# Experts of a routed layer computed on sorted tokens instead of on all tokens for every expert

## The chip, the cores and the metric

One core of one Trainium2 chip runs one program. The time is device microseconds (us) from its first to its last instruction, as the runs report it. The kernel before takes 6748.31 us (median of 3 runs, 6740.82 to 6760.65).

## What is computed

The input has 16 batches of 1024 tokens with 29 features; every token becomes 128 numbers (float32). Two layers follow. Layer 0 is attention with 8 heads of 64 after a group norm, and a small MLP over the channels. Layer 1 is attention with 8 heads of 16, and then the routed part, which is what the change touches:

```python
logits = xf @ switch_w.T + switch_b            # 16 experts
route_probs = max(softmax(logits)); routes = argmax(...)
pos = rank of the token among all tokens (of all batches so far) with its expert
keep = pos < capacity                          # int(1.2 * 16384 / 16)
y = buf @ expert_w[e].T + expert_b[e]          # 128 -> 128, by the token's own expert e
out = where(keep, y[routes, pos], xf) * route_probs
h = h + out
```

## The kernel before

**Batches are pipelined.** The program has five stages: `first` (layer 0 of batch 0), `second` (layer 0 of batch 1 beside layer 1 of batch 0), `loop` (13 passes: layer 0 of batch i+2, layer 1 of batch i+1, and the routed part of batch i), `penult` (the same without a new batch) and `final` (layer 1 of the last batch beside the routed part of the last but one). After `final` the routed part of the last batch runs alone, the tail. The stage `second` has no routed part; otherwise it does what a pass of `loop` does.

**Steps.** An attention unit is one head by one half (512) of the queries; it has 8 steps, each a score product of a key tile (L909, L911), its exponential on ScalarE (L1141) and a share of the products with the values (L930, L931 in layer 0, L946 in layer 1). A pass of `loop` has 32 units, layer 1 and layer 0 in turn, so 256 steps. Everything else is laid beside the steps by hand: each helper is a generator that yields the step at which its next piece is due, and every engine's program is written out in the order of the steps (`Beside.run(step)`). So each engine executes its queue strictly in this order; a wait anywhere holds up all that is behind it on that engine.

**What stands around the change.** The row maxima of the scores are worked out first (products L883 into two banks, reductions on VectorE L1640), turned to a row (L889, L1130), and the row goes into the stack of queries by a DMA from SyncE (`row`, L600), at steps that are multiples of 8. SyncE also issues the stacks of each head: `stack0` three DMAs of 512 KB (L569) at steps 64, 96, 128 and 160 among others, `stack1` five smaller ones at steps 56, 88, 120 and 152. All DMAs are issued by SyncE, on one hardware queue. GpSimd makes the low halves of the probabilities of layer 0 (`lo_parts`, L508), three at kt 2, 4 and 6 of a layer-0 unit and one at kt 0 of the next unit, which TensorE needs from kt 2 of that unit on.

**The routed part** (`switch`, one for each engine) turns and normalizes the tokens (steps 18 to 31), forms the logits, the one-hot `oh` and the rank (`rank`, `place`), and the weight `wgt` = one-hot times kept probability. The expert weights `ewT` (16 x 128 x 128) lie in SBUF throughout. The experts run at steps 64 to 191 of a pass, two pieces every 8 steps:

```python
mm(bank[:, :], mT[:, t * P:(t + 1) * P], ewT[:, 4 * q:4 * q + 4, :]...)      # L869, 32 of them
dve.scalar_tensor_tensor(hm[:, t, :], bank[:, e * P:(e + 1) * P],
                         wgt[:, t, ...], hm[:, t, :], ALU.mult, ALU.add)      # L1630, 128 of them
```

that is, every token tile goes through all 16 experts, and VectorE adds each result times its weight, which is zero for all but one expert. Small products go through two shared PSUM banks (`glue`), whose uses alternate in the order of their steps (`glue_plan`, `use`, `await_filled`, `await_drained`). In `final` a step is shorter, and three expert pieces stand in 16 steps. Step numbers of the routed part are in `switch_slots`; the store of `hm` is at step 191 (124 in `final`), L662 and L665.

## Time and profile before

| | |
|---|---|
| median of 3 runs | 6748.31 us |
| the profiled execution | 6749.96 us, span 6748.1 us |
| granted TensorE clock, mean | 0.948 |
| busy: PE, DVE, ACT, POOL | 90%, 67%, 48%, 37% |
| one pass of `loop` (256 steps) | 402 to 410 us |
| the stage `second` (256 steps) | 371.9 us |
| `final`, then the tail | 185.4 us, 123.3 us |

Stage and step boundaries are the starts of the exponentials L1141 in the trace, one a step: the pass that the rows below use begins at 1987.5 us and ends at 2389.7 us, and its step 64 is at 2095.5, step 80 at 2116.0, step 96 at 2136.2. Of `second`, step 0 is at 396.7, step 64 at 494.8, step 80 at 513.6, step 192 at 660.2. A window that begins and ends at such times shows what a number of steps cost, and the same steps of `second` and of `loop` can be laid side by side.

### The profile page before, as it was taken

How to read it: one execution, taken by the hardware profiler on the slowest of the kernel's cores; microseconds unless marked ns; L12 is line 12 of the kernel's file. 1: busy time of each engine (PE TensorE's matmuls, PEld its weight loads, DVE VectorE, ACT ScalarE, POOL GpSimd, SP SyncE). 2: the span in 40 equal slices, each digit the busy share in tenths (PEclk: the TensorE clock that was granted, in tenths of full speed). 3: DMA queues.
4: the chain of work that ended last, by engine and by line, in shares of the span. 5: the costliest groups of instructions: out<-in, count | busy, mean ns of one | idle time of the engine just before them, and what ended most of it. 6: DMA issues, size and time to landing. Idle time of an engine off the chain costs nothing.

```text
span 6748.1 us, 127182 instructions
## 1 busy us (share of the span) xinstructions
PE 6073.5 (90%) x40167; PEld 4046.7 (60%) x40167; DVE 4525.4 (67%) x11162; ACT 3214.0 (48%) x6321; POOL 2465.6 (37%) x2215
## 2 busy tenths in 40 slices
PE   6789898998989989898998989989898998989986
PEld 4656665656656666665656656666665656656643
DVE  4466676676767767676776767767676776767664
ACT  2345555445444444544545445444544445454541
POOL 2534333433333333333433333333333433333300
PEclk7899999999999999999999999999999999999987
DMA  2121211212222121211212222121211212221110
GB/s 60 41 68 42 59 42 38 64 39 53 49 55 48 40 50 45 59 42 38 64 40 52 49 55 49 40 50 45 59 42 38 64 33 59 49 54 42 25 30 9
DMA packets 98048, 317.03 MB, mean 47 GB/s; under 512 B 27782, under 2 KB 32854, under 8 KB 87126
## 3 DMA queue, kind: packets, MB, share of 16 engines
q1 hardware_dynamic: 97366, 308.41, 19.7%
q8 instruction: 370, 6.06, 0.4%
q14 instruction: 312, 2.56, 0.1%
HBM read 57.19 MB, written 41.94 MB: 15 GB/s over the span
## 4 chain that ended last, share of the span: by engine, by line
issue 47%; POOL 27%; PE 17%; DVE 6%; DMA 1%; POOLq 1%; ACT 1%; SPq 1%; DVEq 0%; ACTq 0%
POOL pr_lo L508 22%; PE bank L883 3%; POOL on L1264 3%; PE bank L911 2%; PE bank L869 2%; PE bank L946 2%; DVE mxh L1640 2%; PE bank L930 1%; DMA stacks<-parts 1%; PE bank L931 1%; DVE z L1428 1%; POOL rs L1235 1%; PE bank L793 1%; PE bank L909 1%; PE bank L956 1%
## 5 line engine op out<-in xcount | busy, mean ns | idle before, releaser
L1640 DVE TENSOR_REDUCE mxh<-bank 128x1 f32<-128x512 f32 x4096 | 2789.9, 687 | 1710.2 <-PE bank L883 1682.2
L1141 ACT ACTIVATE pr<-bank 128x512 f32<-128x512 f32 x4096 | 2419.4, 598 | 2713.8 <-PE bank L911 2669.6
L883 PE MATMUL bank<-stacks 128*128 128x512 f32 x4096 | 2225.5, 544 | 335.2 <-DVE mxh L1640 231.8
L508 POOL TENSOR_TENSOR pr_lo<-pr 128x1024 bf16<-128x1024 f32 x960 | 1824.3, 1901 | 1168.9 <-ACT pr L1141 1168.6
L911 PE MATMUL bank<-stacks 65*128 65x512 f32 (+1 forms) x4096 | 1667.7, 407 | 5.0 <-ACT pr L1141 5.0
L883 PEld LDWEIGHTS bank<-stacks 128*128 128x128 f32 x4096 | 801.3, 196 | 1122.2 <-DVE mxh L1640 804.7
L930 PE MATMUL bank<-v,pr 128*128 128x129 bf16 x8192 | 1079.9, 224 | 54.1 <-POOL pr_lo L508 53.5
L931 PE MATMUL bank<-v,pr_lo 128*128 128x129 bf16 x8192 | 1067.7, 222 | 0.0
L930 PEld LDWEIGHTS bank<-v,pr 128*128 128x128 bf16 x8192 | 787.9, 99 | 348.4 <-issue 306.3
L1264 POOL TENSOR_TENSOR on<-on,o_r 128x128 f32<-128x128 f32 x512 | 235.3, 460 | 2015.7 <-DVE on L1670 2015.6
L911 PEld LDWEIGHTS bank<-stacks 65*128 65x128 f32 (+1 forms) x4096 | 801.6, 196 | 225.0 <-issue 61.7
L909 PE MATMUL bank<-stacks 128*128 128x512 f32 x2048 | 834.4, 407 | 0.2 <-ACT pr L1141 0.2
L931 PEld LDWEIGHTS bank<-v,pr_lo 128*128 128x128 bf16 x8192 | 813.4, 99 | 0.0
L869 PE MATMUL bank<-ewT,mx 128*128 128x512 f32 x1024 | 585.4, 658 | 114.1 <-DVE hm L1630 44.8
L1630 DVE SCALAR_TENSOR_TENSOR hm<-bank,wgt,hm 128x128 f32<-128x128 f32 x2048 | 570.5, 342 | 52.5 <-PE bank L869 52.5
L946 PE MATMUL bank<-pr,v 128*32 128x512 f32 x4096 | 547.0, 609 | 0.0
L909 PEld LDWEIGHTS bank<-stacks 128*128 128x128 f32 x2048 | 402.6, 197 | 131.8 <-ACT pr L1141 77.7
L869 PEld LDWEIGHTS bank<-ewT,mx 128*128 128x128 f32 x1024 | 185.8, 204 | 236.5 <-DVE hm L1630 69.3
L956 PEld LDWEIGHTS bank<-fold,oT 128*128 128x128 f32 x2048 | 272.6, 200 | 60.3 <-ACT oT L1158 46.7
L1041 ACT ACTIVATE parts<-bank,cols 128x512 fp32r<-128x512 f32 x256 | 176.4, 689 | 228.2 <-PE bank L721 228.0
L956 PE MATMUL bank<-fold,oT 128*128 128x32 f32 x2048 | 266.0, 275 | 12.5 <-ACT oT L1158 12.5
L1272 POOL TENSOR_TENSOR on<-on,o_r 128x64 f32<-128x64 f32 x256 | 75.2, 294 | 519.2 <-DVE on L1682 519.1
(171 smaller groups left out, 5070.9 us busy)
## 6 DMA issues: line engine op xcount, KB each, us to landing
stacks<-parts SPq DMA_DIRECT2D x384, 512.0 KB, 6.5
stacks<-parts_d SPq DMA_DIRECT2D x224, 128.0 KB, 3.0
parts_d<-mx SPq DMA_DIRECT2D x16, 1024.0 KB, 4.5
stacks<-parts_d SPq DMA_DIRECT2D x224, 64.0 KB, 2.8
stage<-in_pe SPq DMA_DIRECT2D x16, 512.0 KB, 8.0
stacks<-mrow SPq DMA_DIRECT2D x512, 2.0 KB
parts_d<-on SPq DMA_DIRECT2D x16, 512.0 KB, 5.3
parts_d<-stage SPq DMA_DIRECT2D x16, 512.0 KB, 6.2
```

Source lines behind the costliest of these rows:

```text
L508: return eng.tensor_tensor(low_of(u, kt - 1).rearrange("p a b -> p (a b)"), w, hi, ALU.subtract)
L869: mm(bank[:, :], mT[:, t * P:(t + 1) * P], ewT[:, 4 * q:4 * q + 4, :].rearrange("p e f -> p (e f)"), start=True, stop=True).then_inc(fille ...
L883: mm(maxb[k % 2][:, :], qs[:, t * P:(t + 1) * P], ks[:, g * HALF:(g + 1) * HALF], start=True, stop=True).then_inc(max_filled.sem, 1)
L909: mm(bank[:, :], kA[:, head % 2, kk], qA[:, head % 2, q], start=True, stop=False)
L911: mm(bank[:, :], k_stack(layer, head)[0:last, kk], q_stack(layer, head)[0:last, q], start=(layer == 1), stop=True).then_inc(score_filled.s ...
L930: mm(dst, hi, v0[:, head // 2 % 2, kt, head % 2, 0:w], start=(kt == 0), stop=False)
L931: last = mm(dst, lo, v0[:, head // 2 % 2, kt, head % 2, 0:w], start=False, stop=(kt == T - 1))
L946: last = mm(obank[n % 2][QUAD * r:QUAD * (r + 1), :], v1[:, kt, col:col + QUAD], pr[:, at % 2, kt, :], start=(j == 0), stop=(j == 1))
L956: last = mm(obank[n % 2][:, QUAD * t:QUAD * (t + 1)], oT[:, t * P:(t + 1) * P], fold[:, :], start=True, stop=True)
L1141: act.activation(pr[:, at % 2, kt, :], score[k % 2][:, :], ACT.Exp, scale=SCALES[layer]).then_inc(exp_done.sem, 1)
L1630: ins = dve.scalar_tensor_tensor(hm[:, t, :], bank[:, e * P:(e + 1) * P], wgt[:, t, 4 * q + e:4 * q + e + 1], hm[:, t, :], ALU.mult, ALU.add)
L1640: dve.tensor_reduce(mxh[:, layer, n // 2, n % 2:n % 2 + 1], maxb[k % 2][:, :], AX_X, ALU.max)\
```

## The change

The tokens of a batch are sorted by expert through memory. Every expert gets whole tiles of 128 slots, at most 24 tiles in all. VectorE works out from the counts how many tiles each expert has, where they begin, each token's slot and each tile's expert number (`tables`, `place` + 2). GpSimd scatters the 8 tiles of tokens to `x_sort_d` by 8 indirect DMAs. In 6 groups of 4 tiles, SyncE loads the sorted tokens, TensorE turns them and multiplies each tile by the weights of its one expert, VectorE copies the result and SyncE stores it to `y_sort_d`. GpSimd gathers each token's result by 8 indirect DMAs, and VectorE adds it times the kept probability. The weights now lie in memory (`ew_d`, written at the start); SyncE reads a tile's expert number from SBUF into a register (`value_load`) and loads that expert's 64 KB into a ring of 8. `x_sort` and `y_sort` are the halves of `z`, `y_own` is `mT`.

```diff
@@ switch_slots, of a pass of loop (final: 23, 28, 35, group 42, sums 112 and 118)
+              "logits": 36, "route": 38, "rank": 44, "tables": 46, "place": 54, "wT0": 59, "wT1": 60, "eb0": 62, "eb1": 63, "scatter": 65}
+        group, sums = 74, (148, 156)
+    at.update({f"{name}{g}": group + 12 * g + step for g in range(GROUPS)
+               for name, step in (("load", 0), ("slots", 3), ("product", 5), ("weights", 8), ("store", 9))})
@@ SyncE, before the first load of x
+                sp.dma_start(ew_d.rearrange("e d f -> d e f"), ewT).then_inc(prep_out, 16)
+                for n in range(3):
+                    sp.dma_start(x_sort_d[n * S:(n + 1) * S, :].rearrange("(t p) c -> p t c", p=P),
+                                 stacks1[:, n % 2, 1, :].rearrange("p (t c) -> p t c", t=T).bitcast(F32)).then_inc(prep_out, 16)
@@ SyncE, switch
+                def load_weights(g):
+                    for j in range(4 * g, 4 * g + 4):
+                        e = sp.value_load(tile_ei[0:1, j:j + 1], min_val=0, max_val=E - 1)
+                        sp.dma_start(wring[:, j % 8, :], ew_d[e]).then_inc(weights_in[g % 2].sem, 16)
+                for g in range(2):
+                    yield AT["tables"] + 4 + 2 * g
...
+                    load_weights(g)
+                for g in range(GROUPS):
+                    yield AT[f"load{g}"]
+                    if g == 0:
+                        await_all((scattered.sem, scattered.at(b, 16 * T)))
+                    else:
+                        await_all(drained(seg, f"{pre}slots{g - 1}"))
+                    sp.dma_start(x_sort, x_sort_d[4 * g * P:4 * (g + 1) * P, :].rearrange("(t p) c -> p t c", p=P))\
+                        .then_inc(x_sort_in.sem, 16)
+                    yield AT[f"weights{g}"]
+                    await_all(drained(seg, f"{pre}product{g}"))
+                    if g + 2 < GROUPS:
+                        sp.nop(nofuse=True)
+                        load_weights(g + 2)
+                    yield AT[f"store{g}"]
+                    sp.dma_start(y_sort_d[4 * g * P:4 * (g + 1) * P, :].rearrange("(t p) c -> p t c", p=P), y_sort)\
+                        .then_inc(y_sort_out.sem, 16)
@@ TensorE, switch
-                for n in range(16):
-                    for d in range(2):
...
-                        mm(bank[:, :], mT[:, t * P:(t + 1) * P], ewT[:, 4 * q:4 * q + 4, :].rearrange("p e f -> p (e f)"),
-                           start=True, stop=True).then_inc(filled, 1)
+                for g in range(GROUPS):
+                    yield AT[f"slots{g}"]
+                    te.wait_ge(x_sort_in.sem, x_sort_in.at(b, 16 * (g + 1)))
+                    turn(seg, f"{pre}slots{g}", lambda j: x_sort[:, j, :])
+                    yield AT[f"product{g}"]
+                    te.wait_ge(weights_in[g % 2].sem, weights_in[g % 2].at(b, 64 * (g // 2 + 1)))
+                    bank, filled = use(seg, f"{pre}product{g}", f"{pre}slots{g}")
+                    for j in range(4):
+                        at = g % 2 * HALF + j * P
+                        last = mm(bank[:, j * P:(j + 1) * P], mT[:, at:at + P], wring[:, (4 * g + j) % 8, :], start=True, stop=True)
@@ ScalarE: moves the turned tiles (slots0 to slots5) to mT, one more wait (y_sort_out) at oT0.2.0
@@ GpSimd, switch
+                    if t == 0:
+                        pool.wait_ge(slot_ready.sem, slot_ready.at(b, 1))
+                    pool.indirect_dma_start(x_sort_d, bass.IndirectOffsetOnAxis(slot_i[:, t:t + 1], 0), z[:, t, :], None)\
...
+                    if t == 0:
+                        pool.wait_ge(y_sort_out.sem, y_sort_out.at(b, 16 * GROUPS))
+                    pool.indirect_dma_start(y_own[:, t, :], None, y_sort_d, bass.IndirectOffsetOnAxis(slot_i[:, t:t + 1], 0))\
@@ VectorE, switch: 11 small operations of tables, 4 of slots, then
+                    bank, drained = await_filled(dve, seg, f"{pre}product{g}")
+                    if g > 0:
+                        dve.wait_ge(y_sort_out.sem, y_sort_out.at(b, 16 * g))
+                    dve.tensor_copy(y_sort, bank_tiles(bank)).then_inc(drained, 1)
...
+                        dve.wait_ge(y_own_in.sem, y_own_in.at(b, 16 * T))
+                    ins = dve.scalar_tensor_tensor(hm[:, t, :], y_own[:, t, :], kr[:, t:t + 1], hm[:, t, :], ALU.mult, ALU.add)
-STORE_STEPS = {"loop": 191, "penult": 191, "final": 124}
+STORE_STEPS = {"loop": 163, "penult": 163, "final": 126}
```

## Rows read from the trace of the kernel before

**Rows 1.** Windows, busy time of each engine: stage second, one pass of loop.
```profile
396.70:768.60 371.90, 337.74 (x2370) 228.59 (x2369) 235.46 (x514) 196.19 (x388) 150.67 (x127) 0.97 0.22 51
1987.50:2389.70 402.20, 371.04 (x2510) 249.47 (x2510) 282.21 (x696) 200.78 (x395) 154.10 (x138) 0.97 0.21 49
```
**Rows 2.** Windows, steps 64 to 191: second, then loop.
```profile
494.80:660.20 165.40, 154.02 (x1109) 102.22 (x1108) 102.37 (x222) 88.12 (x182) 71.39 (x61) 0.98 0.23 52
2095.50:2279.70 184.20, 176.66 (x1173) 113.76 (x1172) 135.79 (x352) 88.58 (x181) 70.35 (x59) 0.99 0.21 50
```
**Rows 3.** Windows of 16 steps: second 80, loop 80, second 96, second 128.
```profile
513.60:532.40 18.80, 17.57 (x132) 11.57 (x130) 11.64 (x25) 10.14 (x23) 8.62 (x8) 1.00 0.07 22
2116.00:2136.20 20.20, 20.20 (x140) 13.14 (x139) 15.83 (x41) 10.16 (x23) 8.62 (x8) 1.00 0.07 21
532.40:552.00 19.60, 18.38 (x140) 12.40 (x139) 11.81 (x25) 11.16 (x24) 9.05 (x9) 1.00 0.46 110
574.50:595.70 21.20, 19.43 (x148) 13.36 (x146) 13.61 (x28) 11.21 (x25) 8.61 (x7) 1.00 0.37 76
```
**Rows 4.** Groups of instructions: count, busy us, mean ns, idle before.
```profile
L869 PE MATMUL bank<-ewT,mx 128*128 128x512 f32 x1024 | 585.4, 658 | 114.1 <-DVE hm L1630 44.8 <-DVE parts L1440 26.4 <-DVE stage L1435 22.4
L1630 DVE SCALAR_TENSOR_TENSOR hm<-bank,wgt,hm 128x128 f32<-128x128 f32 x2048 | 570.5, 342 | 52.5 <-PE bank L869 52.5
L1384 DVE COPY ewT<-bank 128x512 f32<-128x512 f32 x4 | 2.5, 682 | 7.3 <-PE bank L693 7.3
L1574 DVE TENSOR_TENSOR lg<-bank,sb_b 128x128 f32<-128x128 f32 x16 | 4.7, 291 | 14.7 <-PE bank L846 14.7
```
**Rows 5.** Timeline of SyncE at steps 96 to 100: start, us, line.
```profile
2136.94 0.67 SPq L600 DMA_DIRECT2D stacks<-mrow  x1
2137.76 3.24 SPq L569 DMA_DIRECT2D stacks<-parts  x3
2141.26 2.17 SPq L638 DMA_DIRECT2D stage<-in_pe  x1
```
**Rows 6.** Windows around these transfers; last columns clock, DMA share, GB/s.
```profile
2139.00:2149.00 10.00, 10.00 (x91) 7.27 (x88) 8.09 (x22) 5.00 (x11) 1.59 (x3) 1.00 0.90 212
2149.00:2157.00 8.00, 8.00 (x51) 4.93 (x50) 6.18 (x18) 4.57 (x9) 5.09 (x4) 1.00 0.00 0
```
**Rows 7.** DMA issues: count, KB each, median us from issue to landing.
```profile
xin<-in_x SPq DMA_DIRECT2D x16, 116.0 KB, 2.1
stacks<-parts_d SPq DMA_DIRECT2D x224, 128.0 KB, 3.0
stage<-in_pe SPq DMA_DIRECT2D x16, 512.0 KB, 8.0
```
**Rows 8.** Timeline of GpSimd around a layer-1 unit: start, us, line.
```profile
2116.24 1.89 POOL L508 TENSOR_TENSOR pr_lo<-pr 128x1024 bf16<-128x1024 f32 x1
2128.00 1.89 POOL L508 TENSOR_TENSOR pr_lo<-pr 128x1024 bf16<-128x1024 f32 x1 [1.32 <-ACT pr L1141]
```
**Rows 9.** Timeline of the start: the load of x, its first reader.
```profile
33.99 0.37 SPq L565 DMA_DIRECT2D xin<-in_x  x1
36.12 1.88 PE L710 MATMUL bank<-tri_sb,xin 128*29 128x128 f32 x8 [8.45 <-DMA xin<-in_x]
```
**Rows 10.** Windows of final (64 steps with experts, 15 without), and the tail's experts.
```profile
6511.60:6608.50 96.90, 81.05 (x376) 40.58 (x376) 69.00 (x186) 41.36 (x81) 2.34 (x8) 1.00 0.06 17
6608.50:6624.80 16.30, 14.26 (x75) 6.29 (x79) 7.64 (x27) 9.47 (x20) 0.59 (x2) 1.00 0.09 33
6658.70:6745.10 86.40, 52.76 (x64) 15.74 (x62) 34.58 (x129) 0.00 (x0) 0.00 (x0) 0.63 0.00 0
```
**Rows 11.** Timeline of the tail: start, us, line; idle before.
```profile
6630.55 3.37 PE L838 MATMUL bank<-wo_sb,mx 128*128 128x128 f32 x16 [0.18 <-ACT mx L1025]
6639.33 1.12 PE L710 MATMUL bank<-tri_sb,z 128*128 128x128 f32 x4 [0.48 <-DVE z L1428]
6652.28 2.18 DVE L1607 SCALAR_TENSOR_TENSOR hm<-z,small,hm 128x128 f32<-128x128 f32 x8
```

More of the change, by code:

```diff
@@ L202, in switch_slots @@
     if kind == "final":
-        at = {"oT1.0": 1, "oT1.1": 2, "attn1.0": 5, "attn1.1": 6, "ln.0": 7, "ln.1": 8, "z.0": 9, "z.1": 10, "zT3.0": 11, "zT3.1": 13, "logits": 15,
-              "route": 16, "rank": 21, "place": 24, "wT0": 29, "wT1": 30, "eb0": 32, "eb1": 33}
-        first = [37 + 16 * m + s for m in range(6) for s in (0, 3, 8)][:16]
+        at = {"oT1.0": 1, "oT1.1": 2, "attn1.0": 5, "attn1.1": 6, "ln.0": 7, "ln.1": 8, "z.0": 9, "z.1": 10, "zT3.0": 11, "zT3.1": 13,
+              "logits": 15, "route": 16, "rank": 21, "tables": 23, "place": 28, "wT0": 33, "wT1": 34, "eb0": 36, "eb1": 37,
+              "scatter": 35}
+        group, sums = 42, (112, 118)
     else:
         at = {"oT1.0": 18, "oT1.1": 19, "attn1.0": 21, "attn1.1": 22, "ln.0": 22, "ln.1": 24, "z.0": 26, "z.1": 28, "zT3.0": 30, "zT3.1": 31,
-              "logits": 36, "route": 38, "rank": 44, "place": 54, "wT0": 59, "wT1": 60, "eb0": 62, "eb1": 63}
-        first = [8 * m for m in range(8, 24)]
-    return {**at, **{f"e{n}.{d}": s + d for n, s in enumerate(first) for d in range(2)}}
-NO_BANK = ("route", "place", "copy", "res0", "gn", "xn", *(f"{name}.{g}" for name in ("ln", "z", "ln1", "z1", "ln2", "z2") for g in range(2)))
+              "logits": 36, "route": 38, "rank": 44, "tables": 46, "place": 54, "wT0": 59, "wT1": 60, "eb0": 62, "eb1": 63, "scatter": 65}
+        group, sums = 74, (148, 156)
+    at.update({f"{name}{g}": group + 12 * g + step for g in range(GROUPS)
+               for name, step in (("load", 0), ("slots", 3), ("product", 5), ("weights", 8), ("store", 9))})
+    return {**at, "gather": sums[0], "sum": sums[1]}
+NO_BANK = ("route", "tables", "place", "scatter", "gather", "sum",
+           *(f"{name}{g}" for name in ("load", "weights", "store") for g in range(6)), "copy", "res0", "gn", "xn", *(f"{name}.{g}" for name in ("ln", "z", "ln1", "z1", "ln2", "z2") for g in range(2)))
 def glue_plan(kind):
@@ L561, in _ @@
                     .then_inc(ones_in, 16)
+            store_prep()
             sp.wait_ge(ones_in, 32)
@@ L652, in segment @@
                     load_x(seg.nxt)
+                if seg.kind == "second":
+                    sp.wait_ge(prep_out, 64)
+                beside = [Beside(switch(seg, "", seg.sw))] if seg.sw else []
                 for step in range(LAST[seg.kind]):
@@ L659, in segment @@
                         load_positions(seg, seg.nxt)
+                    for work in beside:
+                        work.run(step)
                     if seg.sw and step == STORE_STEPS[seg.kind]:
-                        await_drained(sp, seg, "e15.1")
+                        await_all((hm_ready.sem, hm_ready.at(seg.sw, 1)))
                         sp.dma_start(out_v[seg.sw.index()], hm[:, :, :]).then_inc(out_stored.sem, 16)
                 if seg.kind == "final":
-                    await_drained(sp, seg, "f.e15.1")
+                    Beside(switch(seg, "f.", seg.l1)).run(LAST_STEP)
+                    await_all((hm_ready.sem, hm_ready.at(seg.l1, 1)))
                     sp.dma_start(out_v[seg.l1.index()], hm[:, :, :]).then_inc(out_stored.sem, 16)
@@ L1123, in switch @@
                     move_T(seg, f"{pre}wT{g}", xT[0:E, g * HALF:(g + 1) * HALF], E)
+                for g in range(GROUPS):
+                    yield AT[f"slots{g}"]
+                    move_T(seg, f"{pre}slots{g}", half(mT, g % 2))
             def max_rows(seg, name, b, layer, head, g):
@@ L1571, in switch @@
                 top, total, rp, vm, pos, kr, un = (small[:, n, :] for n in range(7))
+                own, tiles, begin, shift = (counts[:, n, :] for n in range(4))
                 yield AT["logits"]
```

129 lines of the change are left out of this document (95 added, 34 removed).

## The prediction

> **What bounds the kernel now.** I read the busy time by stage first. A pass of `loop` keeps TensorE busy for 371 of 402 us, VectorE for 282, GpSimd for 154 [rows 1]; TensorE is the bound, and its queue is in order, so any wait in it is lost unless it falls into the 31 us that are idle. Then I laid `second`, which has no routed part, beside `loop`: 371.9 against 402.2 us. Over steps 64 to 191, where only the experts differ, it is 165.4 against 184.2 us (from 184 to 187 in the passes of `loop`) [rows 2]. That is the ceiling: with the experts gone altogether a pass gains about 20 us; `second` gives about 2 us of it back in the next 16 steps, so I use 19. Busy time would promise more: L869 is 585 us (36.6 a batch) and L1630 570 us (35.7) [rows 4]. But in 16 plain steps four expert products cost 1.4 us of time (20.2 against 18.8), because `second` leaves TensorE 1.2 us idle there [rows 3]. Most of VectorE's relief is worth nothing: it was never the bound.
>
> **Part by part, for one pass of `loop`.**
>
> *Removed*, 32 products and 128 additions: -19 us, as above (bounds -17 and -21).
>
> *TensorE's new work*, 6 groups. Turning four tiles: 16 steps of `second` with two turns more cost 19.6 against 18.8, so 0.4 us a turn. Four products of 128x128 have the form of a value chunk: two of these cost 21.2 - 18.8 = 2.4, so 1.2 us each [rows 3]. 6 x 1.6 = 9.7 us; I take off 3 that falls into idle time, as the experts' did: +6.5.
>
> *VectorE and ScalarE*: six copies of 0.68 and about 15 small operations, the larger ones at 0.29 to 0.6 by L1574 [rows 4]: some 4 us of tables in one place, steps 46 to 57, where the maxima behind them wait: +1.5. Six moves of ScalarE: +0.5. Together with TensorE +8.5; without any wait a pass would gain 10.5.
>
> *Waits for transfers.* This decides. TensorE waits in its queue for the sorted tokens at `slots`, 3 steps after SyncE's `load`, and SyncE has to get there through its own queue. The length of a step here is 1.2 us (18.8 / 16).
>
> Two prices are not in the trace. (a) A register read with its weight DMA. SyncE's issue of a plain DMA takes 0.37 [rows 9], and 0.67 [rows 5]; the read is a round trip, which costs from nothing to the 2.1 us of the smallest load shown [rows 7]. So 0.5 to 2.7 us a pair; I take 1.35 (nearer the bare issue, since no data engine is started for the read), so W = 5.4 us for four. The Trainium skill (DMA: Bandwidth & Descriptors, Latency and other measured facts) states a floor of some 0.6 us for a register load; no run here shows it, and by it W would be 4.4 at least, and the total lower by some 15 us. (b) An indirect DMA on GpSimd, d: from 0.37 (a plain issue of SyncE) to 1.9 (GpSimd's 128x1024 operation [rows 8], which handles far more elements); I take 1.2, the middle, since no row is near it, and keep both ends.
>
> - Group 2 is the worst. Its load is due at step 98, and at step 96 `stack0` issues three DMAs of 512 KB [rows 5]. All go through one queue, and it is full: from 2139 to 2149 us the DMA share is 0.90 at 212 GB/s, then 0.00; these 10 us are the stacks with the 512 KB of positions behind them, which take 8.0 us to land where 128 KB alone take 3.0 [rows 6, 7]. The load of 256 KB, put before the positions, lands at about 2139 + 1.8 MB / 207 KB per us + 0.5 = 2148.3. TensorE wants it at step 101, 2136.2 + 5 x 1.22 = 2142.3: it waits 6 us even if nothing else is late. Further `weights1` is due at step 94, 2.4 us before the stack: W = 5.4 and the store's 0.5 put the row and the stack of step 96 later by about 3 us, and so the load. 9.5 us.
> - Group 1: from `weights0` (82) to `slots1` (89) there are 8.5 us; W + 0.5 (store) + 3.2 (issue and landing) = 9.1: 0.5 us. Groups 4 and 5 stand behind the stacks of 120 and 128: 1 us each. Group 3: nothing.
> - Group 0: from `scatter` (65) to `slots0` (77) there are 14.8 us; 8d + 2.5 (landing) + 3.0 = 15.1: 0.5 us. GpSimd itself has the gap for it: 9.9 us between L508 of step 72's unit and the next [rows 8], against 9.6.
> - Gather (148) to sum (156): 9.6 us; 8d + 2.5 = 12.1, so VectorE stands still for 2.5 and behind it the maxima; TensorE has two banks of them in hand: 1.5 us. The low halves due from step 154 come about 2.5 us late and catch up, since they wait 1.3 us each for exponentials anyway [rows 8].
>
> Together 14 us. A rule speaks against the first of these. The row: 1.5 MB of stacks and 0.5 MB of positions hold the queue for 10 us [rows 6]. The Trainium skill (the same page, Anatomy of one DMA) fits a DMA as 2.0 us plus its bytes at 436 GB/s; by that 1.8 MB would be through in some 4 + 2 us and the wait would be 4 us shorter, the total then by some 55 us. The measured rate is half of that, and I go by it.
>
> One pass: -19 + 8.5 + 14 = +3.5 us; 13 passes: +45. `penult` has no positions to load but is otherwise alike: +4.
>
> *`final`*: 64 steps with experts take 96.9 (24.2 for 16), without 16.3 for 15 (17.4 for 16) [rows 10]: 88 steps give -37. New: 9.7 of TensorE, 1.5 of tables; scatter (35) to `slots0` (45) has 11.3 us against 15.1: 4; gather to sum has 6.8 against 12.1: 5; behind weights and the stacks of 48 and 64: 8. Sum -9.
>
> *Tail*, where nothing hides anything. Before, from `wgt` (6652.3) to 6745.1 us: 93 us [rows 10, 11]. After: tables and slots 2.5, L1607 2.2, scatter 8d + 2.5 = 12.1; each group: issue and landing 3.1, turn 1.1, move 0.6, product 1.7 (half of L838), copy 0.7, store 0.4, hand-overs 0.5 = 8.1, six times 49; four times W = 21.6; then 2.7 + 9.6 + 2.5 + 2.2 = 17. Sum 104: +11.
>
> *Start*: `store_prep` puts 1 + 1.5 MB on the queue in front of the load of x, which TensorE waits for within 2.1 us of its issue [rows 9]. At 207 KB per us this is 12 us, with 2 of issue: +14 (10 to 18). The 48 small memsets of VectorE lie in its wait for the first loads.
>
> **Sum**: 45 + 4 - 9 + 11 + 14 = +65 on the profiled execution's 6750, which stands 2 us above the median: 6815 us.
>
> **Rivals.**
>
> 1. *The transfers hide* (faster). The load of group 2 isn't held up to the end, since the stacks' transfers are done before the positions are, or the steps before it run late enough anyway; register reads are cheap (W = 3). Then the waits are 2 us a pass: -8.5 x 14 = -119; `final` -20, tail 0, start +10: 6621. For it: the ceiling of 20 us is measured, and TensorE loses 17 us of work. Against it: 212 GB/s and the step numbers. The Trainium skill's rate (above) leads the same way, if only to about 6760.
> 2. *GpSimd and SyncE take the place of the wait* (slower still). With W = 9 (2.2 a pair) and d = 1.9: group 0 waits 6, group 1 4, group 2 13, group 4 5, gather 7: 35 us, so +24 a pass. 14 passes +340, tail +40, start +14: 7145. It decides from d above 1.3, where the scatter no longer fits in its 12 steps, and from W above 5, where `weights` reaches the next load. For it: 24 reads and 16 indirect DMAs a pass, each in an in-order queue. Against it: SyncE's issues are short.
> 3. *It doesn't do what it says*: the routed part is off TensorE's path, and the change is worth nothing there. `second` against `loop` speaks against it (19 us). Start and tail alone would give 6773.
>
> **How the numbers follow.** The forecast 0.42 (its own range 6770 to 6900), rival 1 0.32 (6560 to 6750), rival 2 0.18 (6900 to 7400), rival 3 0.08. The bounds of (a) and (b) put a pass between -4 and +35; with the other cases the range is 6600 to 7090. A measurement of this kernel can tell 0.3% (20 us) from no change. Faster by more: rival 1 and a little of the forecast's lower end, 0.33; within: 0.09; slower: 0.58.
>
> **What would show it.** Right: TensorE idle before the turn of group 2 for about 9 us, released by the DMA of `x_sort`; the same turn in groups 0 and 1 with under 1 us; a pass of `loop` of 405 to 412 us; about 20 fewer busy us of TensorE and 25 of VectorE in it; x landing 14 us later at the start; a tail of 104 us after `wgt`. Wrong: no DMA among the releasers of the turns, and steps 64 to 191 in less than 178 us (rival 1); GpSimd's indirect DMAs over 1.5 us each or SyncE over 2 us for a weight tile (rival 2); the load of group 2 landing in 3 us though the stacks are under way.

## The result, and the profile after

The changed kernel takes 6996.52 us (median of 4 runs, 6990.53 to 7008.85) against 6751.26 us of the kernel before beside it: a ratio of 1.0366, 95% interval 1.0345 to 1.0387. It is slower. It lies inside the full range of 6600 to 7090, but outside the forecast's own (6770 to 6900): slower by 245 us where 65 were forecast. By stages (profiled executions, starts of the exponentials as boundaries, us):

| stage | before | after | difference | forecast |
|---|---|---|---|---|
| start | 84.0 | 92.8 | +8.8 | +14 |
| `first` and `second` | 684.6 | 679.1 | -5.5 | 0 |
| 13 passes of `loop` | 13 x 405.3 | 13 x 422.3 | +220 | +45 |
| `penult` | 401.3 | 421.6 | +20.3 | +4 |
| `final` | 185.4 | 174.3 | -11.1 | -9 |
| tail | 123.3 | 131.3 | +8.0 | +11 |

So nearly the whole miss lies in the passes: 16.9 us each where 3.5 were forecast. (The change doesn't touch the work of `first` and `second`; over the kernels below these take 677.5 to 684.4 us, so their -5.5 is scatter.) The windows of the pass that answers to [rows 1 to 3], of the kernel after: the whole pass, steps 48 to 63, steps 64 to 191, steps 80 to 95 (from, to, length, busy time and count of PE, PEld, DVE, ACT, POOL, granted clock, DMA share, GB/s).

```profile
2035.40:2456.20 420.80, 366.15 (x2518) 251.88 (x2518) 264.26 (x596) 204.26 (x401) 170.24 (x154) 0.94 0.26 61
2117.60:2148.40 30.80, 26.23 (x176) 17.70 (x176) 25.03 (x59) 13.77 (x28) 12.86 (x16) 0.96 0.11 31
2148.40:2344.70 196.30, 171.02 (x1181) 116.35 (x1180) 111.31 (x236) 92.03 (x188) 84.86 (x74) 0.92 0.31 74
2172.70:2192.50 19.80, 18.81 (x145) 12.85 (x143) 12.70 (x27) 10.67 (x23) 7.81 (x7) 1.00 0.23 64
```

TensorE is busy 5 us less than before and VectorE 18 less (about 20 and 25 were forecast), and the pass is longer: TensorE's idle time rose from 31 to 55 us. The granted clock adds to it: TensorE was at the lower of its two levels (1.2 GHz) for 697 us of the program before and for 1124 us now, in stretches behind its waits. The calm window of steps 80 to 95 costs 19.8 us, less than the 20.2 with the experts [rows 3]. The table of waits of the kernel after says where the idle time begins (who waits, for whom, us in all, times, longest):

```profile
PE bank L788 <- DMA z<-x_sort_d: 225.8, 68, 12.2
PEld bank L788 <- DMA z<-x_sort_d: 191.8, 54, 12.5
ACT pr L1229 <- remote: 127.2, 37, 6.2
DVE mxh L1771 <- remote: 124.6, 32, 6.7
PE bank L1012 <- POOL pr_lo L541: 86.7, 120, 3.6
```

The first two lines were forecast: the turns wait for sorted tokens. The next two were not: ScalarE and VectorE, which here wait for TensorE's products (the scores, and those whose maxima are taken), stand still up to 6.7 us, and the profile knows no releaser for the wait ("remote" is its word for a signal that it can't place; there is one core). The kernel before has no such line.

*Group 2*, SyncE's queue and then TensorE's, kernel after (start, us, line; idle before in brackets), beside [rows 5]:

```profile
2190.79 3.69 SPq L687 DMA_DIRECT2D wring<-ew_d  x4
2194.53 0.44 SPq L709 DMA_DIRECT2D y_sort_d<-z  x1
2195.09 0.71 SPq L641 DMA_DIRECT2D stacks<-mrow  x1
2195.98 3.27 SPq L610 DMA_DIRECT2D stacks<-parts  x3
2199.37 2.31 SPq L701 DMA_DIRECT2D z<-x_sort_d  x1
2201.94 2.13 SPq L679 DMA_DIRECT2D stage<-in_pe  x1
```
```profile
2206.65 1.12 PE L788 MATMUL bank<-tri_sb,z 128*128 128x128 f32 x4 [7.43 <-DMA z<-x_sort_d]
```

Four register reads with their weight DMAs take 4.6 us (forecast 5.4, bounds 2 to 10.8): the 3.69 us of the row begin with the first DMA, and the read in front of it begins at 2189.85. A read takes 0.27 us (median of 384), a pair 1.12. The load comes behind the three stacks, as worked out, and TensorE stands for it. The signs that were named for this came true: before the turn of group 2 TensorE waits 7.4 us a pass for `x_sort`, before that of group 0 not at all, before that of group 1 0.9 us.

*The scatter*, GpSimd, VectorE and ScalarE of the kernel after, at steps 64 to 72. Here is the new thing:

```profile
2146.50 1.89 POOL L541 TENSOR_TENSOR pr_lo<-pr 128x1024 bf16<-128x1024 f32 x1
2148.56 1.09 POOL L1387 DMA_INDIRECT x_sort_d<-z,slot_i  x1 [0.17 <-issue]
2149.95 0.97 POOL L1387 DMA_INDIRECT x_sort_d<-z,slot_i  x1 [0.30 <-issue]
...
2155.03 0.96 POOL L1387 DMA_INDIRECT x_sort_d<-z,slot_i  x1 [0.30 <-issue]
2158.78 0.40 POOL L1353 TENSOR_TENSOR on<-on,o_r 128x128 f32<-128x128 f32 x1 [2.80 <-DVE on L1801]
```
```profile
2152.63 0.69 DVE L1771 TENSOR_REDUCE mxh<-bank 128x1 f32<-128x512 f32 x1 [2.03 <-issue]
2157.42 0.69 DVE L1771 TENSOR_REDUCE mxh<-bank 128x1 f32<-128x512 f32 x1 [4.11 <-remote]
```
```profile
2153.01 0.60 ACT L1229 ACTIVATE pr<-bank 128x512 f32<-128x512 f32 x1 [2.08 <-PE bank L993]
2157.46 0.60 ACT L1229 ACTIVATE pr<-bank 128x512 f32<-128x512 f32 x1 [3.85 <-remote]
```

Six indirect DMAs follow each other 1.27 us apart (d, forecast 1.2). While they run, VectorE and ScalarE both wait some 4 us for products of TensorE and go on within 0.04 us of each other. VectorE's product was the first of these, done at 2154.12 by the profile, 3.3 us before VectorE goes on; the two last products of this kind, which start at 2154.19 and 2154.42, were done 2.6 us before:

```profile
2153.65 0.47 PE L965 MATMUL bank<-stacks 128*128 128x512 f32 x1
2154.19 0.39 PE L965 MATMUL bank<-stacks 128*128 128x512 f32 x1
2154.42 0.40 PE L993 MATMUL bank<-stacks 128*128 128x512 f32 x1
```

GpSimd itself is not what they wait for: it is idle for 2.80 us at the end, waiting for VectorE.

The trace also holds the times at which the engines' signals (semaphore increments) were seen, and they say what is late. TensorE's are seen 0.01 us behind the product (median). Here five of them, of products that ended from 2153.84 to 2154.82, are seen between 2157.37 and 2157.50, one every 0.03 us: held, then let go together. Each of the 4096 reductions of VectorE (L1771) belongs to one product of TensorE (L965), so they can be paired. In the kernel after, 41 of them start more than 1 us after both their product and their engine were ready, 6.5 us at most. In the kernel before the longest such delay is 0.1 us. (The ends of products are modelled by the profile, but 0.1 and 6.5 us come from the same model.)

*Start* and *tail*, kernel after: SyncE's stores, then TensorE's first wait, which was 8.45 us [rows 9]. From the last `wgt` (6885.8 us) to the end (6988.7) it is 102.9 us; 104 were forecast.

```profile
33.38 0.45 SPq L592 DMA_DIRECT2D ew_d<-pr  x1
33.87 5.36 SPq L594 DMA_DIRECT2D x_sort_d<-stacks  x3
39.27 1.79 SPq L606 DMA_DIRECT2D xin<-in_x  x1
```
```profile
44.88 1.88 PE L788 MATMUL bank<-tri_sb,xin 128*29 128x128 f32 x8 [16.72 <-DMA xin<-in_x]
```

### The profile page after: what moved, and what is told of

Its sections match the earlier page's. It is cut to its first block, busy times and chain, and to the rows that moved or that the text cites. A ratio compares the mean times of both kernels' runs of the same rounds, so it can differ in the third digit from the quotient of the medians.

```text
span 6988.7 us, 127660 instructions
## 1 busy us (share of the span) xinstructions
PE 5958.0 (85%) x40295; PEld 4084.1 (58%) x40295; DVE 4223.4 (60%) x9610; ACT 3271.9 (47%) x6417; POOL 2725.3 (39%) x2471
## 3 DMA queue, kind: packets, MB, share of 16 engines
q0 software_dynamic: 8192, 16.79, 0.9%
## 4 chain that ended last, share of the span: by engine, by line
issue 46%; POOL 29%; PE 14%; DVE 5%; DMA 2%; SPq 2%; ACT 1%; POOLq 1%; another core or an unknown queue 0%; DVEq 0%; ACTq 0%
POOL pr_lo L541 21%; PE bank L965 3%; POOL on L1353 2%; PE bank L993 2%; DVE mxh L1771 2%; POOL x_sort_d L1387 1%; PE bank L1028 1%; POOL mx L1395 1%; PE bank L1012 1%; DMA stacks<-parts 1%; DVE z L1540 1%; PE bank L1013 1%; PE bank L871 1%; POOL rs L1324 1%; PE bank L991 1%
## 5 line engine op out<-in xcount | busy, mean ns | idle before, releaser
L1771 DVE TENSOR_REDUCE mxh<-bank 128x1 f32<-128x512 f32 x4096 | 2773.9, 687 | 2147.4 <-PE bank L965 1974.9
L965 PE MATMUL bank<-stacks 128*128 128x512 f32 x4096 | 2122.3, 519 | 507.3 <-DVE mxh L1771 387.0
L993 PE MATMUL bank<-stacks 65*128 65x512 f32 (+1 forms) x4096 | 1712.1, 418 | 11.2 <-DMA stacks<-mrow 5.0
L965 PEld LDWEIGHTS bank<-stacks 128*128 128x128 f32 x4096 | 823.5, 201 | 1284.6 <-DVE mxh L1771 965.5
L1012 PE MATMUL bank<-v,pr 128*128 128x129 bf16 x8192 | 1104.4, 227 | 88.8 <-POOL pr_lo L541 86.7
L1013 PE MATMUL bank<-v,pr_lo 128*128 128x129 bf16 x8192 | 1092.4, 225 | 2.7 <-issue 2.7
L993 PEld LDWEIGHTS bank<-stacks 65*128 65x128 f32 (+1 forms) x4096 | 827.4, 202 | 174.5 <-issue 37.4
L991 PE MATMUL bank<-stacks 128*128 128x512 f32 x2048 | 852.1, 416 | 9.4 <-ACT pr L1229 5.3
L991 PEld LDWEIGHTS bank<-stacks 128*128 128x128 f32 x2048 | 412.4, 201 | 86.0 <-ACT pr L1229 41.8
L788 PE MATMUL bank<-tri_sb,z 128*128 128x128 f32 x768 | 146.9, 323 | 237.5 <-DMA z<-x_sort_d 225.8
L1038 PEld LDWEIGHTS bank<-fold,oT 128*128 128x128 f32 x2048 | 290.3, 210 | 61.7 <-ACT oT L1246 45.1
L1107 ACT ACTIVATE mx<-bank 128x512 f32<-128x512 f32 (+1 forms) x256 | 152.7, 597 | 368.5 <-PE bank L788 367.5
L1038 PE MATMUL bank<-fold,oT 128*128 128x32 f32 x2048 | 281.2, 284 | 12.5 <-ACT oT L1246 12.5
L788 PEld LDWEIGHTS bank<-tri_sb,z 128*128 128x128 f32 x768 | 106.0, 165 | 297.6 <-DMA z<-x_sort_d 191.8
```

Of the source, the lines that this page charges most:

```text
L788: last = te.transpose(bank[0:rows_, j * P:(j + 1) * P], src(j), ident)
L965: mm(maxb[k % 2][:, :], qs[:, t * P:(t + 1) * P], ks[:, g * HALF:(g + 1) * HALF], start=True, stop=True).then_inc(max_filled.sem, 1)
L991: mm(bank[:, :], kA[:, head % 2, kk], qA[:, head % 2, q], start=True, stop=False)
L993: mm(bank[:, :], k_stack(layer, head)[0:last, kk], q_stack(layer, head)[0:last, q], start=(layer == 1), stop=True).then_inc(score_filled.s ...
L1012: mm(dst, hi, v0[:, head // 2 % 2, kt, head % 2, 0:w], start=(kt == 0), stop=False)
L1013: last = mm(dst, lo, v0[:, head // 2 % 2, kt, head % 2, 0:w], start=False, stop=(kt == T - 1))
```

## Experiments

Since all engines run in the order of the steps, I lay the start times of the exponentials, step by step and as a mean over the 13 passes, beside those of the kernel before without its experts. A cost then shows as a jump at a step and stays. "At 96 to 104" means: between these steps.

### 1. The ceiling, and what the indirect DMAs add to it

```diff
 e1_b_noexperts, from the kernel before
-                for n in range(16):          (TensorE's L869, VectorE's L1630)
 e2_b_noexp_indirect: e1, and on GpSimd, waited for by no other engine
+                first, second = (35, 112) if seg.kind == "final" else (65, 148)
+                for t in range(T):           (two a step)
+                    pool.indirect_dma_start(ind_d, ...ind_i[:, t:t + 1]..., ind_sb[:, t, :], None)
+                for t in range(T):           (the same from ind_d to ind_sb at second)
```

> The kernel before without its expert products and their additions (L869, L1630), the rest of the routed part kept; it leaves the expert outputs out of the result. It measures the ceiling. If second against loop is a fair picture (my forecast's 19 us a pass), steps 64 to 191 take about 165 us and the whole about 6751 - 14 x 19 - 40 (final) - 85 (tail) = 6360 us. If TensorE's relief is partly taken back by later waits (rival), a pass gains 10 us or less and the whole is above 6480.

> The same kernel with 8 indirect scatters and 8 indirect gathers on GpSimd at steps 65 and 148 of a pass (35 and 112 in final), to and from a buffer of their own that no engine reads; nothing waits for them. Theory hold-up: indirect DMAs in flight hold up TensorE's completions by themselves (the trace of the changed kernel shows exponentials and maxima idle 3 to 6 us with no releaser, about twice a batch): 8 us a pass and some slow clock behind, so 110 to 200 us above e1. Theory waits: only what waits for the transfers costs time, GpSimd has room: within 20 us of e1.

Without the 32 products and 128 additions: 6360.57 us (ratio 0.9417, 0.9402 to 0.9433), a pass 18.3 us shorter than before (forecast 19). With 16 indirect DMAs a batch beside it, of data that nobody reads: 6543.39 (0.9685, 0.9665 to 0.9704), a pass 12.0 us longer again. The ledger has two jumps, +4.6 us at 64 to 72 and +7.3 at 152 to 160, the places of the two eights. The waits of this kernel show the lines without a releaser, which e1 has not:

```profile
ACT pr L1141 <- remote: 135.7, 47, 5.3
DVE mxh L1640 <- remote: 137.2, 33, 6.7
```

So it is the indirect DMAs that hold the engines up, whatever their data are for. Paired as above, 37 reductions of e2 are held for over 1 us, the longest for 6.4 us. In e1 none is held for more than 0.1 us.

### 2. The changed kernel without its indirect DMAs, and with earlier loads

```diff
 e3_a_noindirect
-                    pool.indirect_dma_start(x_sort_d, ...)   and the gather's; their signals are given at once
 e4_a_loads_early, SyncE's switch
-               for name, step in (("load", 0), ("slots", 3), ...
+    at.update({f"load{g}": group + (12 * g - 7 if g else 0) for g in range(GROUPS)})
+                    if g + 1 < GROUPS:
+                        yield AT[f"load{g + 1}"]
+                        load(g + 1)          (ahead of weights g and store g)
```

> The changed kernel without its 16 indirect DMAs a batch; their semaphores are raised by GpSimd itself, so the sorted tokens are not the batch's. Theory hold-up: it gains what e2 loses to e1, 8 us a pass or more, plus VectorE's wait for the gather (2 to 3 us): 6996 - 14 x 11 - 30 (final and tail) = about 6810. Theory waits: it gains only VectorE's wait and the late scatter, 3 to 4 us a pass: about 6925.

> The changed kernel with the load of group g+1 issued 2 steps after the turn of group g (7 steps earlier than in the change), so ahead of the weights, the store and the stacks of steps 96, 120 and 128. Theory waits for sorted tokens: the 11 us at steps 100 to 104 and the 4 us at 136 to 140 go, with the slow clock behind them: 14 x 14 = -190, about 6800. Rival (a wait moved, not removed: the queue is the bound and the stacks or the rows come later): under 5 us a pass, above 6930.

e3: 6892.52 us (1.0218, 1.0201 to 1.0235), 104 us less than the kernel after. That is nearer to the second theory (6925) than to the first (6810). The hold-up is gone nevertheless: no wait without a releaser is left, the wait for group 2 is (10.6 us at 96 to 104), and so is that of group 5 (5.8 at 136 to 144). e4 is the counterpart: 6765.76 us (1.0018, 1.0008 to 1.0029). Both jumps are nearly gone (1.3 and 0.9 us are left), a pass is 15.0 us shorter, and the waits for sorted tokens fall from 225.8 us to these (e4, the whole program):

```profile
PE bank L795 <- DMA z<-x_sort_d: 29.9, 6, 12.3
```

One edit of seven steps in SyncE's queue thus takes back nearly all that the change had cost. The jumps of +4.7 at 64 to 72 and +7.9 at 152 to 160 stay in e4. In e3 they are -0.1 and +2.1, the latter from the sum at step 156, where the kernel after has 3.5 and 8.0. Of these 9.5 us e3 gives 3 back behind step 160, and its pass is 6.5 us shorter where the first theory wanted 8 or more and VectorE's wait on top.

### 3. What of an indirect DMA holds the engines up

Four kernels from e1, with 16 operations of GpSimd a batch each:

```diff
 e5_b_noexp_gpsimd_busy: additions, at the steps of e2
+                        link(seg, pool.tensor_tensor(ind_sb[:, 4:7, 0:110], ind_sb[:, 0:3, 0:110], ind_sb[:, 0:3, 0:110], ALU.add))
 e6_b_noexp_plain_dma: plain addresses, at the steps of e2
+                    pool.dma_start(ind_d[t * P:(t + 1) * P, :], ind_sb[:, t, :])
 e7_b_noexp_ind_quiet: e2 at other steps
+                first, second = (35, 112) if seg.kind == "final" else (81, 177)
 e8_b_noexp_ind_spread: e2, one in three steps
+                    yield first + (t if seg.kind == "final" else 3 * t)
```

> The kernel before without its experts (6360.6) with 16 additions of 128x330 on GpSimd a batch, about 1.0 us each, at the steps where the run with indirect DMAs (6543.4) had its 16: same time taken on GpSimd, no DMA. Theory QUEUE (the indirect DMAs cost by the 0.96 us that each holds GpSimd, behind which low parts and normalizations are late): 6520 to 6560, the same +12 us a pass. Theory PATH (what holds up TensorE, ScalarE and VectorE is how the indirect DMAs reach the rest of the chip, not GpSimd's time): 6360 to 6410, at most 3 us a pass, and no waits of ScalarE or VectorE without a releaser.

> The same 16 transfers of 64 KB a batch at the same steps, issued by GpSimd too, but with plain addresses in place of indices. If any transfer issued by GpSimd at these steps holds the engines up (PATH, all kinds): 6500 to 6550. If only the indirect ones do, by reading indices and writing 128 addresses each (PATH, indirect): 6365 to 6400. QUEUE expects the issue time on GpSimd times 16 in ratio to 0.96 us: with 0.3 us each 6400 to 6430.

> The kernel before without its experts with the 16 indirect DMAs moved from steps 65 and 148 to steps 81 and 177 of a pass, packed as they were. At 81 and 177 GpSimd is busy 7.8 of 20 and 11 of 24 us (15 of 24 and 16 of 27 at the old places, with the indirect ones in it) and at 177 no stack is under way. QUEUE: the low parts have slack there, 6400 to 6460. PATH with contention for the DMA engines: half of it left, 6440 to 6480. PATH without: as before, 6530 to 6560.

> The kernel before without its experts with the 16 indirect DMAs of a batch one every three steps from steps 65 and 148 (in the last segment one a step), in place of two a step. QUEUE: 0.96 us at a time fits between the low parts, 6370 to 6420. PATH with a fixed hold-up for each DMA (0.75 us each of the 12 us a pass): 6530 to 6560. PATH with a hold-up that builds up only where they queue: 6380 to 6440, which this run does not tell from QUEUE, but the run with additions does.

e5: 6375.99 us (0.9445, 0.9428 to 0.9462), no jump, but the additions took 0.74 us each, too short a stand-in. e6: 6359.64 (0.9424, 0.9401 to 0.9446): the same bytes by plain DMAs of GpSimd cost nothing, though an issue takes 0.55 us. They go through the same queue (`q0 software_dynamic`) in as many packets, 8192 in both kernels, and follow each other more closely, 0.53 us apart. So it is neither the queue nor the packets. e7: 6573.74 (0.9729, 0.9710 to 0.9749): the quiet steps don't help; the jumps are +6.5 at 80 to 88 and +6.7 at 176 to 184, and a third kind of wait without a releaser appears:

```profile
DVE mxh L1640 <- remote: 166.6, 52, 5.2
ACT pr L1141 <- remote: 101.1, 38, 5.9
ACT on L1025 <- remote: 55.6, 21, 5.0
```

e8: 6399.67 us (0.9474, 0.9458 to 0.9491), 0.9 us at the scatter's 24 steps and 0.6 at the gather's, and no such wait. So moving the eights to other steps doesn't help, and taking them apart does.

### 4. The cure in the changed kernel

```diff
 e9_a_spread, from the changed kernel; e10_a_early_spread, the same from e4
-"scatter": 65}
-        group, sums = 74, (148, 156)
+"scatter": 59}
+        group, sums = 74, (148, 173)
+                    yield AT["scatter"] + (t // 2 if seg.kind == "final" else 2 * t)
+                    yield AT["gather"] + (t // 2 if seg.kind == "final" else 3 * t)
+STORE_STEPS = {"loop": 180, "penult": 180, "final": 126}
 e11_a_all: e10 (scatter from 57), and
-            store_prep()                      (before the load of x)
+                    store_prep()              (after load_positions of the first segment)
-                        yield AT["place"] + 3 + t // 4
+                    yield AT["eb1"] + 2 + t // 2 * (1 if seg.kind == "final" else 2)   (8 additions to hm)
```

> The changed kernel (6996.5) with its indirect DMAs apart and nothing else: in all segments but the last, the 8 of the scatter one every two steps from step 59 (before: two a step from 65), the 8 of the gather one every three steps from 148 (before: two a step), the sum at 173 and the store of the output at 180. Theory: closely packed indirect DMAs cost about 4.7 us at steps 64 to 72 and 8 us at 152 to 160 of each of 14 passes; apart they cost 2 of these 12.7: 6996 - 14 x 10.5 = 6850, range 6820 to 6890. Rival: the hold-up is that of a scatter that reads memory which the other engines use (not in the experiments without experts) and stays: 6980 to 7000.

> Both cures in one: loads seven steps earlier (6765.8 alone) and the indirect DMAs apart as in the kernel beside it. If they add up: 6766 - 147 = 6620, range 6590 to 6650, which is faster than the kernel before by 2%. If the earlier loads had taken part of the hold-up already, 6680.

> The kernel with both cures, its 1.5 MB of stores at the start issued after xin's load instead of ahead of it (start +8.8 us against the kernel before), and the eight additions to hm moved from steps 57 and 58 to 65 to 71, behind the biases of the experts. Start: -8 to -10. Steps 56 to 64, where VectorE is busy 25.0 of 30.8 us: -1 to -3 us in each of 14 passes. In all 6575 to 6605; if VectorE does not set the pace there, 6610.

e9: 6858.19 us (1.0164, 1.0140 to 1.0188; expected 6850). e10: 6615.45 (0.9809, 0.9791 to 0.9828; expected 6620). e11: **6551.55** (0.9713, 0.9697 to 0.9728), 2.9% faster than the kernel before and faster than was expected: the later additions and the scatter two steps earlier gave 3.7 us a pass against e10, where 1 to 3 were expected, and the start 8.7. The whole pass and steps 64 to 191 of e11, and its waits for sorted tokens:

```profile
1941.70:2338.10 396.40, 357.41 (x2518) 246.35 (x2518) 261.93 (x596) 203.33 (x401) 170.49 (x154) 0.96 0.27 64
2053.80:2225.30 171.50, 160.18 (x1182) 108.72 (x1180) 113.46 (x245) 91.17 (x188) 83.45 (x72) 0.99 0.34 83
```
```profile
PE bank L796 <- DMA z<-x_sort_d: 28.4, 7, 10.2
```

The same instructions as in the kernel after, and 24.8 us less in these 128 steps; the clock is 0.99 where it was 0.92. The ledger, us behind the kernel before without experts (mean of 13 passes):

| step | before | after | e3 | e4 | e9 | e10 | e11 |
|---|---|---|---|---|---|---|---|
| 56 | -0.3 | 1.6 | 1.6 | 1.9 | 2.0 | 1.9 | 2.3 |
| 64 | -0.3 | 5.2 | 4.4 | 4.6 | 2.1 | 1.9 | 1.3 |
| 72 | 1.1 | 8.7 | 4.3 | 9.3 | 3.6 | 3.8 | 1.6 |
| 96 | 3.4 | 10.7 | 6.4 | 10.3 | 6.8 | 6.2 | 3.4 |
| 104 | 3.7 | 21.7 | 17.0 | 11.6 | 17.7 | 7.5 | 4.6 |
| 136 | 9.4 | 22.8 | 18.0 | 12.3 | 18.8 | 8.2 | 5.3 |
| 144 | 11.2 | 28.1 | 23.8 | 13.2 | 24.0 | 9.1 | 6.2 |
| 152 | 11.5 | 28.1 | 23.8 | 13.2 | 24.0 | 9.1 | 6.2 |
| 160 | 12.5 | 36.1 | 25.9 | 21.1 | 24.0 | 9.1 | 6.2 |
| 256 | 18.3 | 35.2 | 28.8 | 20.3 | 25.6 | 10.9 | 7.2 |

### 5. Rate, bytes, or GpSimd's queue

```diff
 e12_b_noexp_ind_each_step: e2, one a step
+                    yield first + t
 e13_b_noexp_busy_long: e5 with longer additions
+ind_sb[:, 8:13, 0:115], ind_sb[:, 0:5, 0:115], ind_sb[:, 0:5, 0:115]
 e14_b_noexp_ind_quarter: e2 with a quarter of the bytes
+ind_sb[:, t, 0:P // 4]                       (both directions; ind_d is 1024 x 32)
 e15_b_noexp_ind_fours: e2 in runs of four
+                        yield first + t // 2 + (14 if t > 3 and seg.kind != "final" else 0)
```

> The kernel before without its experts with one indirect DMA a step from steps 65 and 148, between the packed run (two a step, 6543.4) and the run with one in three steps (6399.7). A hold-up that needs a queue of them: they are issued 2.5 us apart instead of 1.3, so nearly all gone, 6400 to 6430. A hold-up that falls in proportion to their rate: 6460 to 6480.

> The kernel before without its experts with 16 additions of 128x575 on GpSimd a batch in place of the 128x330, which took 0.74 us each instead of the 1.0 wanted. At the rate of those rows they take some 1.25 us, the spacing at which the packed indirect DMAs follow each other. QUEUE (GpSimd's time alone holds the others up): 6520 to 6560, as with the packed indirect DMAs (6543.4). PATH (something that only indirect DMAs do): 6380 to 6430, the low part behind the second eight being some 3 us late at step 156.

> The packed indirect DMAs of the run at 6543.4 with rows of 32 elements in place of 128: as many instructions, indices and addresses, a quarter of the bytes. If the bytes hold the engines up (memory or transfer rate): a quarter of 183 us left, 6400 to 6420. If it is the number of indirect DMAs or of their addresses: 6530 to 6550.

> The packed indirect DMAs in fours: two a step from steps 65, 81, 148 and 164 in place of eight at 65 and eight at 148. Hold-up in proportion to their number, however they lie: 6540. Hold-up that builds up along a run of them (a backlog that one in 2.5 us doesn't make at steps 65 to 72, but one in 1.27 does): four build up less than half of it each, 6380 to 6440.

| | us | ratio, interval | at 64-72 | at 152-160 | at 160-168 |
|---|---|---|---|---|---|
| e2, eights, 64 KB each | 6543.39 | 0.9685, 0.9665 to 0.9704 | 4.6 | 7.3 | -0.1 |
| e14, eights, 16 KB | 6515.21 | 0.9643, 0.9615 to 0.9671 | 4.4 | 6.7 | -0.2 |
| e15, fours, 64 KB | 6394.98 | 0.9471, 0.9449 to 0.9492 | 0.9 | 0.0 | 0.5 |
| e12, one a step, 64 KB | 6478.08 | 0.9599, 0.9582 to 0.9617 | -0.1 | 0.0 | 6.6 |
| e13, additions | 6434.61 | 0.9535, 0.9515 to 0.9554 | 0.2 | 0.0 | 5.7 |

e14 is decisive on bytes: a quarter of them costs nearly the same. e15 is decisive on how it grows: the same number in runs of four costs 1.9 us a pass instead of 12.0 (a few waits without a releaser are left, 3.1 us at most; a reduction is held for up to 2.4 us behind its product). e13 tells GpSimd's own time apart. Its additions took 1.14 us each, eight in 10 us as the indirect DMAs, and at 64 to 72, where e2 loses 4.6 us, cost nothing. The same eight steps in windows: e1, e2, e13.

```profile
2037.70:2047.00 9.30, 9.30 (x84) 7.31 (x84) 5.61 (x11) 5.04 (x11) 1.26 (x2) 0.85 0.65 135
```
```profile
2067.80:2081.00 13.20, 10.78 (x84) 8.31 (x84) 5.54 (x11) 5.03 (x11) 8.83 (x10) 0.79 0.72 160
```
```profile
2051.00:2061.00 10.00, 10.00 (x84) 7.80 (x84) 5.42 (x11) 4.99 (x11) 9.37 (x10) 0.78 0.71 145
```

But GpSimd's queue has a price of its own, at the gather. In e13 the low parts behind the second eight come late, and TensorE waits for the last of them. GpSimd and then TensorE, e13:

```profile
2160.24 7.25 POOL L1291 TENSOR_TENSOR ind_sb<-ind_sb 128x575 f32<-128x575 f32 x6
2167.66 0.40 POOL L1259 TENSOR_TENSOR on<-on,o_r 128x128 f32<-128x128 f32 x1 [0.16 <-POOL ind_sb L1291]
2168.02 2.37 POOL L1291 TENSOR_TENSOR ind_sb<-ind_sb 128x575 f32<-128x575 f32 x2
2170.54 5.59 POOL L509 TENSOR_TENSOR pr_lo<-pr 128x1024 bf16<-128x1024 f32 x3 [0.16 <-POOL ind_sb L1291]
2176.35 1.89 POOL L509 TENSOR_TENSOR pr_lo<-pr 128x1024 bf16<-128x1024 f32 x1
```
```profile
2178.37 0.29 PE L924 MATMUL bank<-v,pr 128*128 128x129 bf16 x1 [4.93 <-POOL pr_lo L509]
```

The three low parts at 2170.54 run without a gap, and the fourth ends at 2178.2; TensorE has stood 4.93 us for it. The jump of e12 at the same steps is this one too (there TensorE waits 5.08 us for L515 at 2188.14). My expectation of e12, a hold-up in proportion to the rate, gave the right total for the wrong reason.

This price and the hold-up hide each other in e2, since both fall on the steps behind the gather. Its 12.0 us a pass are therefore not the hold-up's alone: e13 loses 4.9 a pass without any indirect DMA, and 7.1 are what indirect DMAs add to GpSimd's time.

e12 says one thing more. Its indirect DMAs were not 2.5 us apart, as I had expected: a step is some 1.2 us long, so one a step is about as close as they can follow each other. At the gather six stand 1.25 to 1.54 us apart, nearly as in e2 (GpSimd, e12):

```profile
2170.24 1.02 POOL L1303 DMA_INDIRECT ind_sb<-ind_d,ind_i  x1 [0.39 <-issue]
2171.56 0.96 POOL L1303 DMA_INDIRECT ind_sb<-ind_d,ind_i  x1 [0.30 <-issue]
2172.82 0.95 POOL L1303 DMA_INDIRECT ind_sb<-ind_d,ind_i  x1 [0.31 <-issue]
2173.79 0.41 POOL L1265 TENSOR_TENSOR on<-on,o_r 128x128 f32<-128x128 f32 x1
2174.36 0.99 POOL L1303 DMA_INDIRECT ind_sb<-ind_d,ind_i  x1 [0.16 <-issue]
2175.66 0.95 POOL L1303 DMA_INDIRECT ind_sb<-ind_d,ind_i  x1 [0.30 <-issue]
2176.91 0.95 POOL L1303 DMA_INDIRECT ind_sb<-ind_d,ind_i  x1 [0.30 <-issue]
2177.88 1.90 POOL L515 TENSOR_TENSOR pr_lo<-pr 128x1024 bf16<-128x1024 f32 x1
```

Yet no reduction of e12 is held for more than 0.3 us. What differs is how many indirect DMAs stand in GpSimd's queue with no other operation between them, in `loop` and `penult`:

| kernels | longest unbroken run | reductions held over 1 us | longest, us |
|---|---|---|---|
| after, e2, e4, e7, e14 | 6 | 37 to 57 | 5.2 to 6.5 |
| e15 | 4 | 23 | 2.4 |
| e12 | 3 | 0 | 0.3 |
| e8, e9, e10, e11 | 2 | 0 | 0.4 |
| e6, plain DMAs | 6 | 0 | 0.1 |

So the eights were really six and then two, with a small operation (L1265 or its like) between them. Spacing alone doesn't explain e12. The length of the unbroken run orders all the kernels in these stages, but no run changed it alone, so this is a reading of the traces and not a tested cause. And it isn't enough by itself: in `final`, where layer 0 doesn't run beside them, seven and eight stand unbroken at 1.27 us in the kernel after, in e9 and in e11 too, and none of TensorE's signals is over 1 us late there. In e2, e7, e14 and e15 some signals are 2.2 to 2.8 us late there.

## Why the prediction missed

**The pass, term by term**, in us above the kernel before without experts, by the jumps of the kernel after in the ledger:

| term | forecast | found |
|---|---|---|
| the ceiling (experts gone) | -19 | -18.3 |
| tables and slots, 48 to 64 | 1.5 | 5.2 |
| scatter (group 0 doesn't wait), 64 to 72 | 0.5 | 3.5 |
| group 2, 96 to 104 | 9.5 | 11.0 |
| group 5, 136 to 144 | 1 | 5.3 |
| gather and sum, 152 to 160 | 1.5 | 8.0 |
| all else (six groups' work, groups 1, 3, 4) | 8.5 | 2.2 |
| sum | +3.5 | +16.9 |

**Where it was right.** The ceiling; group 2, by the very mechanism (behind the stacks in SyncE's queue); d, 1.2 against 1.27; the tail, 104 against 102.9; `final`, -9 against -11.1. The Trainium skill (DMA: Bandwidth & Descriptors, Anatomy of one DMA) has its 436 GB/s from single DMAs issued by GpSimd. By it the wait for group 2 would have been about 4 us shorter; the 11.0 us bear out the 207 KB per us of [rows 6] instead.

**The step that failed** is the sum of the waits, "Together 14 us" a pass, and in it the terms of the scatter and the gather: the 16 indirect DMAs were priced by GpSimd's time alone. In the two places that I put at 0.5 and 1.5 us stand 3.5 and 8.0. Two errors lie in this. The hold-up of TensorE's signals had no term at all (7.1 of e2's 12.0 us a pass). And GpSimd's time was priced too low at the gather: the low halves don't "catch up", they cost 5.7 us there in e13. That GpSimd "has the gap" for the scatter was right: the additions of e13 cost 0.2 us at 64 to 72. Set apart in the same kernel (e9), the indirect DMAs make the pass 9.6 us shorter: by step 80 e9 stands at 6.0 us where the kernel after stands at 9.9 and e3, which has none, at 5.6, and between 152 and 160 it loses nothing. No row of before could show it, since that kernel has no indirect DMA; but the bounds on d were bounds on GpSimd's time, not on what it does to the others. They should have been bounds on the pass.

**The mis-sized terms.** Group 5: SyncE issues the stacks of step 128 and then `store4` and the load behind them, the mechanism of group 2 once more, which I gave 1 us. Tables and slots: VectorE is busy 25.0 of the 30.8 us of steps 48 to 63, its heaviest window, so what is added there seems to delay the maxima nearly in full (argued, no run takes the tables alone away); the slots had no term at all. Against these stand 6.3 us that I charged for the groups' work and for waits of groups 1 and 4: the groups' work fits TensorE's idle time nearly whole, and group 4 doesn't wait. W was 4.6, not 5.4, which was worth little, because what is late at group 2 is the load behind the stacks. The start cost 8.8, not 14: issued after the load of x (e11) it costs nothing (84.1 us against 84.0). `penult` went the way of the passes.

**The rivals.** Rival 1 is out: the transfers do not hide, though e4 shows that seven steps suffice to hide them. Rival 2 named GpSimd and SyncE and its range (6900 to 7400) holds the result, but neither of its prices came true: W = 4.6 where it wanted 9, d = 1.27 where it wanted 1.9. GpSimd's queue, which it named, is a real cost only at the gather, 5.7 us in e13; in the packed kernels it doesn't show beside the hold-up. Rival 3 is out: e11 shows the change worth 194 us once its transfers lie well.

**What stays open.** The runs show that the hold-up comes from indirect DMAs in a row, that additions of the same length and plain DMAs of the same queue and bytes don't cause it, that a quarter of the bytes leaves most of it (10.3 us a pass against 12.0), and that it comes at all four places of a pass that were tried, but not always in `final`. In the passes, runs of four bring little of it and runs of three or fewer none. Whether the length of the unbroken run decides or something that goes with it was not tested; an experiment would put one small operation behind every third indirect DMA of e2 and change nothing else. What in the chip is busy then was not seen. The Trainium skill (SBUF — State Buffer, SBUF: two separate sides) holds that compute and DMA can't slow each other at the ports of SBUF, but for GpSimd's and VectorE's shared port, and that TensorE and ScalarE wait on no one there. e2 shows a delay that this rule doesn't tell of: VectorE sees TensorE's products up to 6.4 us late, with no data in common with the DMAs. Whether any port is behind it, no run says. The same page's warning on DMAs from GpSimd (the DVE blocks DMA trap) is about their being late, not about their making others late. A backlog somewhere on the way of the signals would fit the five that came together, but that is argued, not shown.

## To carry to other kernels

- An operation that the old profile doesn't show has two prices: the time on its own engine, and what it does to the others. Take it into the old kernel with its work removed, at the planned steps and waited for by nobody; that one run (e2) gave 12 us a pass that no row of before could. A stand-in that takes the engine's time alone (e13) then divides the two prices, 4.9 and 7.1 us.
- Put indirect DMAs apart, where the plan allows it: one every two or three steps instead of eight at two a step. In the passes of e8 that came out mostly 3 to 5 us apart, never more than two in a row, and cost 2.1 us a pass instead of 12.0. One a step ends the hold-up too, but in this plan GpSimd is then late for its other work (e12, 6.6 us behind the gather).
- A load whose data are ready belongs in the queue ahead of the transfers that are merely due at that time. Ask which place in the queue, not which step.
